# Routing between the attention tasks of bodies 1 to 3, token rows sent from body 4 on, on one NeuronCore

## The chip, the cores and the metric

The kernel runs on one core of a Trainium2 chip. The core has five engines that run side by side: TensorE (PE in the profile, its weight loads PEld), VectorE (DVE), ScalarE (ACT), GpSimd (POOL), and SyncE (SP), which here only issues DMAs. The metric is the device time of one execution in microseconds (us), as a median of several runs; less is better.

## The reference, cut to what matters

The input is 8 sequences of 512 tokens with 128 features. After a layer norm, an attention layer (32 query heads, 16 key/value heads, ALiBi bias, causal) and a mixture of experts read the same normed tokens; the result is x + attention * silu(experts). The experts part decides where each token goes from eight gate logits:

```python
gate_logits = x @ gate_w + gate_b
topk_vals, topk_idx = jax.lax.top_k(gate_logits, K)     # K = 2 of E = 8
topk_w = jax.nn.softmax(topk_vals, axis=-1)
comb = jnp.sum(onehot * topk_w[..., None], axis=2)
h = gelu(jnp.einsum('btd,edf->ebtf', x, w1) + b1)
y = jnp.einsum('ebtf,efd->ebtd', h, w2) + b2
output = jnp.einsum('ebtd,bte->btd', y, comb)
x = x + attention(xn) * silu(output)
```

The kernel does not compute all eight experts for every token. It sorts tokens into blocks of 256 slots, each block of one expert, computes the blocks, and gathers each token's two results.

## The kernel before, in words

**Stages.** There is a preamble (loads, layer norm, transposes, weights split in high and low halves, gate logits), then 32 attention bodies, then the expert blocks, then 32 more attention bodies, and the final sum. A body is two key/value heads of one sequence. In the first 32 bodies the tokens also go out to memory in slot order (`slot_x`): one tile of 128 tokens a body. The experts read `slot_x` and write `slot_y`; the last 32 bodies fetch rows of `slot_y`.

**Order.** No scheduler decides anything at run time: each engine runs its own list in order, and semaphores join them. `ORDER` (L70) gives for each engine and half a table of tasks (name, body offset, place in per cent of a window). `one_window` (L315) runs one window: a task with offset 1 works for the next body. `enter_bodies` (L338) runs the two windows before the first, `run_bodies` (L344) the rest, the first four and the last four written out and those between as a loop of two windows, `leave_bodies` what remains.

**Tasks.** On PE, M are twelve rough score products a body, from which DVE takes row maxima (B, twelve a body, `peaks`, L1382); C turns these shifts (L887); S are the ten groups of scores (L904 to L913); P the ten groups of values (L936 to L940); K, Q, V and O are projections. ACT takes exponentials (E, L1180), copies shifts (C, L1169) and splits high halves; DVE subtracts to get low halves (Q, K, V, A) and divides by the sum (N). POOL subtracts for each exponential group its low half (L, `lo_part`, L781: one instruction of 128x512), which P of the same group waits for. Group 9 of a body is L9 on POOL and P9 on PE. The O projection lags by two bodies.

**Choosing and routing.** While the windows before body 0 run, DVE does the top-2 choice in three steps behind B1, B3 and B5 (`choose`, L1365). Then, between `enter_bodies` and the first window: PE multiplies the choices with a triangle and with ones to rank the tokens of each expert (33 matmuls, L991 and L994, into columns of PSUM bank 4, which the values tasks use later); ACT does one exponential (L1233) with an activation table load before and one behind; DVE waits for the exponential and the ranks and does the routing in 27 instructions without a break (L1478 to L1519), each followed by a wait for its own end (`small`). It ends with `routed`. PE's first values task waits for `routed` (L920).

**Sending rows.** For a tile of 128 tokens, ACT copies the high halves (R, `send_hi`, L1199), POOL subtracts the low halves and copies the two slot numbers of each token (I0, I1, `send_ready`), and issues two indirect DMAs (D0, D1, `send`, L758). `sent_with` (L463) says which tiles belong to a body: tile n-2 in bodies 2 to 29, tiles 28 and 29 in body 30, 30 and 31 in body 31. There are two buffers, by the tile's parity; R and I0 wait until the last tile of their buffer has landed. R stands at 72 per cent of window n-2, I0 at 82 of window n-2, I1 at 34, D0 at 62 and D1 at 75 of window n-1.

## Time and profile before

| | |
|---|---|
| median of 3 runs | 1255.06 us (1253.67 to 1255.94) |
| the profiled execution: time, span | 1253.06 us, 1251.1 us |
| busy, share of the span | PE 92%, DVE 80%, ACT 75%, POOL 70% |
| share of time of the DMA queue of the hardware rings | 54.7% |
| mean granted TensorE clock | 0.981 |

The page of the profile also has the span in 40 slices, groups of instructions by line with their mean duration and the wait before them, and DMA issues. A timeline row is: start in us, length in us, engine, line, operation, output<-input and shapes, count, and in brackets the idle time of the engine just before, with what ended it. A row of busy time gives, for one stretch, how long each engine was busy in it.

### The profile page before, as it was taken

The numbers are of one execution on the slowest core, as the hardware profiler recorded it, in microseconds if no ns is written. First come the engines' busy times: TensorE is split into PE (matmuls) and PEld (weight loads), VectorE is DVE, ScalarE is ACT, GpSimd is POOL, SyncE is SP. The second block draws the span as 40 slices with busy tenths as digits, with TensorE's granted clock in tenths as the row PEclk, the third lists the DMA queues.
The fourth block names the chain that finished last, engine by engine and source line by source line (L and its number), as shares of the span: only waits on it lengthen the run. The fifth ranks groups of instructions, "written<-read, shape, count | busy, mean of one in ns | idle before, by whom it ended". The sixth has DMA issues, their size and how long they took to land. (4 is left out here: it accounts for less than half of the span.)

```text
span 1251.1 us, 52908 instructions
## 1 busy us (share of the span) xinstructions
PE 1154.0 (92%) x17226; PEld 912.5 (73%) x17226; DVE 1005.5 (80%) x3099; ACT 939.0 (75%) x1807; POOL 878.3 (70%) x1086
## 2 busy tenths in 40 slices
PE   2579999999999999987999779999999999999994
PEld 0357777777777777766888657777777777777873
DVE  8778888888888888764777648888888888888885
ACT  2468888888888888775666458888888888888884
POOL 9048888888888888875000058888888888888885
PEclk9989999999999999999999979999999999999997
DMA  8326666666666666644433456555555555555663
GB/s 243 158 57 144 143 147 151 143 143 144 144 144 144 144 143 143 147 107 86 87 90 86 94 129 141 136 135 134 134 134 134 134 134 134 134 134 134 138 139 95
DMA packets 286161, 165.28 MB, mean 132 GB/s; under 512 B 174994, under 2 KB 274674, under 8 KB 285428
## 3 DMA queue, kind: packets, MB, share of 16 engines
q1 hardware_dynamic: 281972, 155.63, 54.7%
q0 software_dynamic: 4096, 8.40, 2.3%
q8 instruction: 59, 0.97, 0.3%
q14 instruction: 34, 0.28, 0.1%
HBM read 15.76 MB, written 16.78 MB: 26 GB/s over the span
## 5 line engine op out<-in xcount | busy, mean ns | idle before, releaser
L781 POOL TENSOR_TENSOR t_lo<-stage 128x512 f16<-128x512 f32 x640 | 654.4, 1038 | 148.7 <-ACT stage L1180 144.5
L1392 DVE CUSTOM_DVE_ANT_0 stage<-ps,kmask 128x512 bf16<-128x512 f32 (+3 forms) x1024 | 466.2, 488 | 110.7 <-PE ps L878 91.9
L1180 ACT ACTIVATE stage<-ps,slope 128x512 f32<-128x512 f32 (+1 forms) x768 | 456.8, 620 | 126.8 <-PE ps L913 80.7
L904 PE MATMUL ps<-q_st,k_st 128*128 128x256 f16 (+3 forms) x1024 | 302.5, 301 | 4.0 <-DMA k_st<-stage 1.8
L936 PE MATMUL outs<-v_sp,stage 128*128 128x65 f16 x2560 | 283.3, 194 | 12.2 <-DVE stage L1422 9.0
L938 PE MATMUL outs<-v_sp,stage 128*128 128x64 f16 x2560 | 283.1, 194 | 0.0
L940 PE MATMUL outs<-v_sp,t_lo 128*128 128x65 f16 x2560 | 283.0, 194 | 0.0
L878 PE MATMUL ps<-k_st,stage 128*128 128x512 f16 (+3 forms) x1024 | 252.8, 304 | 14.9 <-DVE spread L1392 7.6
L936 PEld LDWEIGHTS outs<-v_sp,stage 128*128 128x128 bf16 x2560 | 239.4, 98 | 21.5 <-issue 11.2
L938 PEld LDWEIGHTS outs<-v_sp,stage 128*128 128x128 bf16 x2560 | 236.5, 98 | 8.9 <-issue 0.3
L940 PEld LDWEIGHTS outs<-v_sp,t_lo 128*128 128x128 f16 x2560 | 236.5, 98 | 0.0
L905 PE MATMUL ps<-q_st,k_st 128*128 128x128 f16 x1024 | 224.0, 219 | 0.0
L908 PE MATMUL ps<-q_st,k_st 67*128 67x384 f16 (+2 forms) x768 | 211.5, 275 | 0.0
L1169 ACT CAST q_st<-ps 1x512 f16<-1x512 f32 x256 | 147.9, 578 | 32.5 <-PE ps L887 27.2
L913 PE MATMUL ps<-late_q,late_k 66*128 66x134 f16 (+1 forms) x640 | 136.0, 212 | 0.0
L904 PEld LDWEIGHTS ps<-q_st,k_st 128*128 128x128 f16 x1024 | 100.4, 98 | 34.7 <-issue 14.3
L734 POOL COPY slot_now<-slot_of 128x1 uint32 (+1 forms) x128 | 23.2, 183 | 144.6 <-DMA slot_y<-stage 144.6
L878 PEld LDWEIGHTS ps<-k_st,stage 128*128 128x128 f16 x1024 | 84.3, 98 | 53.0 <-issue 24.3
L1125 ACT ACTIVATE stage<-ps,qscale 128x512 f16<-128x512 f32 x128 | 88.5, 691 | 44.9 <-PE ps L816 36.9
L905 PEld LDWEIGHTS ps<-q_st,k_st 128*128 128x128 f16 x1024 | 100.4, 98 | 17.2 <-issue 0.6
L908 PEld LDWEIGHTS ps<-q_st,k_st 67*128 67x128 f16 x768 | 74.8, 97 | 51.7 <-issue 1.9
L1422 DVE TENSOR_TENSOR stage<-outs,stage 128x512 f16<-128x512 f32 x128 | 88.0, 687 | 21.7 <-ACT stage L1160 21.7
(205 smaller groups left out, 2702.1 us busy)
## 6 DMA issues: line engine op xcount, KB each, us to landing
k_st<-stage SPq DMA_DIRECT2D x256, 128.0 KB, 2.4
q_st<-stage SPq DMA_DIRECT2D x256, 128.0 KB, 2.4
q_st<-stage SPq DMA_DIRECT2D x256, 64.0 KB, 2.1
k_st<-stage SPq DMA_DIRECT2D x128, 64.0 KB, 2.1
slot_y<-stage SPq DMA_DIRECT2D x40, 128.0 KB, 2.0
X<-in_L_attn_inputs SPq DMA_DIRECT2D x8, 512.0 KB, 8.0
slot_x<-att SPq DMA_DIRECT2D x2, 2048.0 KB, 8.7
wx_raw<-in_L_ffn_w SPq DMA_DIRECT2D x64, 64.0 KB
```

What stands on the lines that cost most here:

```text
L781: pool.tensor_tensor(t_lo[r], t_p[r], upper(t_p[r]), ALU.subtract).then_inc(s[f"lo{u % NG}"], 1)
L878: mm = pe.matmul(M_ps[h][:, c0:c0 + w], q_raw[sl][:, 0, i * P:(i + 1) * P], k_st[par][sl][:, 2 + h, 0:w], start=True, stop=True)
L904: pe.matmul(d, k[:, 0, at], q[:, 0, seen], start=(c0 == 0), stop=False, skip_group_check=True)
L905: pe.matmul(d[:, 0:P], k[:, 1, at], q[:, 1, at], start=False, stop=True, skip_group_check=True)
L908: pe.matmul(d[:, P:], k[far, 1, at], q[far, 1, (kt + 1) * P:SEQ], start=False, stop=True, skip_group_check=True)
L913: pe.matmul(d, late_k[late, :], late_q[late, LATE:P].unsqueeze(1).to_broadcast([P - LATE - 1, len(first), P - LATE]), start=False, stop=Tr ...
L936: pe.matmul(d, p_hi, v[:, with_one], start=(opens and i == kt), stop=False, skip_group_check=True)
L938: pe.matmul(d[:, OUT_COL[sl]:OUT_COL[sl] + DH], p_hi, v[:, lo], start=False, stop=False, skip_group_check=True)
L940: mm = pe.matmul(d, t_lo[r][:, c], v[:, with_one], start=False, stop=(closes and i == QT - 1), skip_group_check=True)
L1169: ins = act.copy(q_st[sl][h][DH:DH + 1, 1, :], M_ps[0][SHIFT[h]:SHIFT[h] + 1, :])
L1180: e = act.activation(t_p[r][:, c0:c1], S_ps[u % 2][:, c0:c1], ACT.Exp, scale=slope[:, bass.ds(pair_index(n) * 2 * SLOTS + sl * 2 + h, 1)])
L1392: ins = dve.tensor_tensor_reduce(junk[h][:, c0:c0 + w], M_ps[h][:, c0:c0 + w], kmask[:, SEQ - w:SEQ], -1.0 / 1024, 3e38, ALU.add, ALU.min, ...
```

## The change

1. `run_bodies`: the first half now writes out windows 0 to 17 and 30, 31 and loops over 18 to 29 (before: written out 0 to 3 and 28 to 31). The second half writes out its first four and last two.
2. The 33 rank matmuls are called on PE behind V0 of body 1 in window 0 (`ranks`). ACT, behind E4 of body 0, copies ranks and totals out of PSUM (`keep_ranks`); PE's first values task waits for these copies (`kept`) and no more for `routed`.
3. The 27 routing instructions on DVE are cut in eight steps (`route`), run behind B3 and B5 of body 1, N0 of body 0, B3 and B5 of body 2, N0 of body 1, B3 and B5 of body 3. They read the copies, not PSUM.
4. The activation table for Exp is loaded once, before the odd tiles are normed, and not around L1233.
5. Rows are sent from body 4 on: tile 0 with body 4, one a body, two in bodies 7, 10, 13 and 16 (the first of them through a third buffer), so that from body 17 on tile n goes with body n and body 31 sends one. R stands at 0 of the window and no more at 72.

```diff
-            ("E0", 0, 4), ("E1", 0, 8), ...
+            ("R0", 2, 0), ("E0", 0, 4), ("E1", 0, 8), ...
-            ("E7", 0, 71), ("R0", 2, 72), ("A0", 0, 76), ...
+            ("E7", 0, 71), ("A0", 0, 76), ...
-                if "Y" in tasks and name in CHOICE:
-                    tasks["Y"](n, 0, CHOICE[name])
-        CHOICE = {"B1": 0, "B3": 1, "B5": 2}
+                if "Y" in tasks and isinstance(n, int) and (name, n) in FIRST_ONES[engine_name]:
+                    tasks["Y"](FIRST_ONES[engine_name].index((name, n)))
+        FIRST_ONES = {"DVE": [("B1", 0), ("B3", 0), ("B5", 0), ("B3", 1), ("B5", 1), ("N0", 0), ("B3", 2), ("B5", 2),
+                              ("N0", 1), ("B3", 3), ("B5", 3)],
+                      "PE": [("V0", 1)], "ACT": [("E4", 0)]}
-            start, end = lo + 2 * UNROLL, hi - 2 * UNROLL
+            start, end = lo + (max(TWICE) + UNROLL if lo == 0 else 2 * UNROLL), hi - UNROLL
+        rank_of, total_of = L, t1[:, 0, :]
-        def sent_with(n):
+        FIRST_SENT, TWICE = 4, (7, 10, 13, 16)
+        def sent_with(n, par):
             if not isinstance(n, int):
-                return [n - UNROLL]
-            return [t for t in range(NT) if min(t + UNROLL, HALF - UNROLL + (t - NT) // 2 + UNROLL) == n]
+                return [(n, par, (n - FIRST_SENT) // UNROLL)]
+            if n < FIRST_SENT:
+                return []
+            t = n - FIRST_SENT + len([b for b in TWICE if b <= n])
+            more = [(t - 1, UNROLL, TWICE.index(n))] if n in TWICE else []
+            return more + [(t, n % UNROLL, (n - FIRST_SENT) // UNROLL)]
...
-                    pe.wait_ge(s["routed"], 1)
+                    pe.wait_ge(s["kept"], 2)
...
+            def keep_ranks(_):
+                act.wait_ge(s["ranked"], 1)
+                act.copy(rank_of, ps[4][...]).then_inc(s["kept"], 1)
+                act.copy(total_of, ps[4][...]).then_inc(s["kept"], 1)
```

The steps of `route` (the instructions are those of L1478 to L1519 in their order): step 0 is L1478 to L1480; 1 waits for `kept` and is L1483 to L1489; 2 is L1491 to L1494; 3 is L1497 to L1499; 4 is L1500 to L1505; 5 the four of L1508 and L1509; 6 is L1511 and L1512; 7 is L1514 to L1519.

## Rows read from the trace of the kernel before

**Rows 1.** Two stretches: length, busy PE, PEld, DVE, ACT, POOL, PE clock, DMA.
```profile
189.70:220.80 31.10, 30.92 (x490) 24.73 (x488) 27.00 (x87) 26.03 (x52) 27.01 (x33) 1.00 0.66 152
82.65:115.00 32.35, 31.10 (x484) 23.50 (x483) 26.81 (x92) 27.26 (x52) 25.83 (x31) 1.00 0.60 125
```

**Rows 2.** Timeline, window 1: K0 and end of B6 on DVE, M8 on PE.
```profile
101.66 0.69 DVE L1407 SCALAR_TENSOR_TENSOR stage<-ps,stage 128x512 f16<-128x512 f32 x1 [0.48 <-ACT stage L1133]
...
102.87 0.09 DVE L1392 DVE_READ_ACCUMULATOR2_ANT spread<- 128x1 f16 x1
...
103.10 0.38 PE L878 MATMUL ps<-k_st,stage 128*128 128x128 f16 x2
```

**Rows 3.** Timeline of POOL: a window with one tile, and one with two.
```profile
504.19 1.01 POOL L758 DMA_INDIRECT slot_x<-row_now,slot_now  x1 [0.15 <-issue]
...
506.45 0.98 POOL L758 DMA_INDIRECT slot_x<-row_now,slot_now  x1 [0.17 <-issue]
...
509.60 4.02 POOL L781 TENSOR_TENSOR t_lo<-stage 128x512 f16<-128x512 f32 x4
...
538.35 1.01 POOL L758 DMA_INDIRECT slot_x<-row_now,slot_now  x1 [0.15 <-issue]
...
543.15 0.96 POOL L758 DMA_INDIRECT slot_x<-row_now,slot_now  x1 [0.31 <-issue]
```

**Rows 4.** Timeline of PE: the first matmul of P9 after the one-tile window.
```profile
511.71 0.19 PE L936 MATMUL outs<-v_sp,stage 128*128 128x65 f16 x1
```

**Rows 5.** Timeline of PE around the routing.
```profile
62.96 0.42 PE L991 MATMUL outs<-chosen,tri 128*128 128x264 f16 x1
...
66.32 0.38 PE L904 MATMUL ps<-q_st,k_st 128*128 128x512 f16 x1
...
76.28 0.59 PE L887 MATMUL ps<-ident,spread 128*128 128x128 f16 x4 [8.71 <-DVE spread L1392]
```

**Rows 6.** Timeline of ACT: its V0 task, once a body.
```profile
112.16 0.60 ACT L1140 ACTIVATE v_sp<-ps 128x512 f16<-128x512 f32 x1
...
143.13 0.60 ACT L1140 ACTIVATE v_sp<-ps 128x512 f16<-128x512 f32 x1
...
251.90 0.64 ACT L1140 ACTIVATE v_sp<-ps 128x512 f16<-128x512 f32 x1
...
500.60 0.64 ACT L1140 ACTIVATE v_sp<-ps 128x512 f16<-128x512 f32 x1
...
534.79 0.63 ACT L1140 ACTIVATE v_sp<-ps 128x512 f16<-128x512 f32 x1
...
555.85 0.63 ACT L1140 ACTIVATE v_sp<-ps 128x512 f16<-128x512 f32 x1
```

**Rows 7.** Timeline of DVE, routing instructions.
```profile
64.83 0.18 DVE L1478 TENSOR_SCALAR top<-top 128x32 f32<-128x32 f32 x1 [0.94 <-ACT top L1233]
...
67.93 1.02 DVE L1494 TENSOR_SCALAR per_e<-per_e 128x8 f32<-128x8 f32 x1
68.99 1.28 DVE L1497 TENSOR_TENSOR wx_lo<-wx_lo,per_e 128x320 f32<-128x320 f32 x1
...
75.14 0.23 DVE L1519 TENSOR_TENSOR slot_of<-slot_of,slot_bits 128x64 uint32<-128x64 uint32 x1
```

**Rows 8.** Timeline of POOL in the same stretch.
```profile
67.88 2.04 POOL L781 TENSOR_TENSOR t_lo<-stage 128x512 f16<-128x512 f32 x2 [36.37 <-ACT stage L1180]
```

**Rows 9.** Timeline of ACT: the second R in body 31's pair.
```profile
544.88 0.30 ACT L1204 CAST row_now<-mix 128x128 f16<-128x128 f32 x1 [4.25 <-DMA slot_x<-row_now,slot_now]
```

**Rows 10.** Who PE waited for from 560 to 572 us: total, times, longest.
```profile
PE outs L936 <- POOL t_lo L781: 1.5, 3, 0.9
```

**Rows 11.** Timeline of POOL: the low half of a tile that is sent.
```profile
507.46 0.44 POOL L746 TENSOR_TENSOR row_now<-mix,row_now 128x128 f16<-128x128 f16 x1
```

**Rows 12.** DMAs that write or read `slot_x`, from issue to landing.
```profile
DMA to landing us min/median/max: 3.0/3.4/12.8
```

**Rows 13.** Timeline of ACT: E0 and E1 at a window's start.
```profile
510.39 1.35 ACT L1180 ACTIVATE stage<-ps,slope 128x512 f32<-128x512 f32 x2 [0.62 <-PE ps L913]
```

More of the change, by code:

```diff
@@ L420, in weights_split, with over_e @@
             eng.wait_ge(s["wlo"], len(SPLITS))
+        L, t1, one1, L2, one2, cw = (lg[:, i, :, :] for i in range(6))
+        rank_of, total_of = L, t1[:, 0, :]
+        def over_e(a):
+            return a.unsqueeze(2).to_broadcast([P, NT, E])
+        ev = eidx[:, :].unsqueeze(1).to_broadcast([P, NT, E])
         RANK = E * FC
@@ L736, in send_ready @@
             def send_ready(n, par, k):
-                for i, t in enumerate(sent_with(n)):
-                    at = t % UNROLL if isinstance(t, int) else par
+                for t, at, used in sent_with(n, par):
                     if isinstance(t, int) and (t, k) == (0, 0):
@@ L750, in send @@
             def send(n, par, k):
-                for t in sent_with(n):
-                    at = t % UNROLL if isinstance(t, int) else par
+                for t, at, _ in sent_with(n, par):
                     pool.wait_ge(s["ready0"], t * 2 + 2)
@@ L1199, in send_hi @@
             def send_hi(n, par, _):
-                for t in sent_with(n):
-                    at = t % UNROLL if isinstance(t, int) else par
-                    need(act, f"sent{at}", t // UNROLL * 32)
+                for t, at, used in sent_with(n, par):
+                    need(act, f"sent{at}", used * 32)
                     act.copy(row_now[at][:, 0:D], mix[:, bass.ds(t, 1), :].rearrange("p a d -> p (a d)"))\
@@ L1221, in _ @@
             roots(1, QT, NT)
+            act.preload_act_table(ACT.Exp)
             act.wait_ge(s["norm"], 1)
@@ L1474, in _ @@
             dve.wait_ge(s["attz"], 1)
-            enter_bodies("DVE", {**tasks, "Y": lambda n, _, k: choose(k)}, 0, HALF)
-            dve.wait_ge(s["topexp"], 1)
-            small(dve.tensor_scalar(top[:, 6, :], top[:, 5, :], WS, WS, ALU.mult, ALU.add))
-            small(dve.reciprocal(top[:, 6, :], top[:, 6, :]))
-            small(dve.tensor_tensor(top[:, 7, :], top[:, 6, :], top[:, 5, :], ALU.mult))
-            blocks, first, end, first_slot = (per_e[:, i, :] for i in range(4))
-            small(dve.tensor_scalar(ecmp[:, :, :], ecmp[:, :, :], 0.0, None, ALU.is_gt))
@@ L1484, in _ @@
-            dve.wait_ge(s["ranked"], 1)
-            total = ps[4][:, RANK + NT * E:RANK + (NT + 1) * E]
-            over = scratch[:, 0:TOK // BLK * E].rearrange("p (e j) -> p e j", e=E)
-            small(dve.tensor_tensor(over, total.unsqueeze(2).to_broadcast([P, E, TOK // BLK]), steps[:, :, :],
-                                    ALU.is_gt))
-            small(dve.tensor_reduce(blocks, over, AX_X, ALU.add))
-            before = scratch[:, 0:E * E].rearrange("p (e f) -> p e f", e=E)
-            small(dve.tensor_tensor(before, blocks.unsqueeze(1).to_broadcast([P, E, E]), ecmp[:, :, :], ALU.mult))
@@ L1492, in _ @@
-            small(dve.tensor_reduce(first, before, AX_X, ALU.add))
-            small(dve.tensor_tensor(end, first, blocks, ALU.add))
-            small(dve.tensor_scalar(first_slot, first, float(BLK), None, ALU.mult))
-            ended = scratch[:, :].rearrange("p (b e) -> p b e", e=E)
-            small(dve.tensor_tensor(ended, block_no[:, :, :], end.unsqueeze(1).to_broadcast([P, NBLK, E]), ALU.is_ge))
-            small(dve.tensor_reduce(blk_f[:, :], ended, AX_X, ALU.add))
-            small(dve.tensor_scalar(blk_f[:, :], blk_f[:, :], E - 1.0, None, ALU.min))
@@ L1523, in _ @@
             dve.wait_ge(s["zeros"], 16 * ZERO_DMAS)
-            run_bodies(dve, "DVE", tasks, 0, HALF)
+            run_bodies(dve, "DVE", {**tasks, "Y": lambda k: route(k - CHOICES)}, 0, HALF)
             leave_bodies("DVE", tasks, 0, HALF, late=LATE_O)
```

114 lines of the change are left out of this document (72 added, 42 removed), and 4 rows, old and new, of the table ORDER.

## The prediction, as written before the result

> **What bounds the kernel now.** I read the busy times by stretch first. In the middle of the first half two bodies take 31.1 us, in which PE is busy 30.9, DVE 27.0, POOL 27.0 and ACT 26.0 [rows 1]. So in a settled body every microsecond that PE waits is lost, and the next two engines have some 2 us of slack a body. That slack isn't free to use, because the lists are fixed: in window 1 DVE ends B6 at 102.96 and PE starts M8, which needs it, at 103.10 [rows 2]. DVE delivers 0.1 to 0.2 us ahead of its use, so a delay there comes out on PE nearly one for one. POOL is as tight at one place: it ends four L groups (L8, L9, L0, L1, one every 1.0 us) from 509.60 on, so L9 ends at 511.6, and P9 starts at 511.71 [rows 3, 4]. Two places stand out from the settled state: the start, where PE idles 8.71 us until 76.28 because DVE is routing [rows 5], and the last windows of the first half, where the bodies get longer [rows 6]. The change touches both, and moves work into the tight bodies for it.
>
> **Part 1, the start.** PE ranks from 62.96 to 66.32 (3.36 us), does S0, M11 and S1, and idles until C1 at 76.28 [rows 5]. C1 needs B10 and B11, which stand behind the routing on DVE. With the routing gone, DVE is free at 63.9 (where it begins to wait for L1478), PE goes from 62.96 straight to S0, S1 takes the place of the ranks, and C1 comes at about 65.4: it needs M11 behind S0 (0.9 us at the slow clock, twice the time it has behind the ranks), then B11 and S1. That is 10.9 us earlier. The removed table loads are what lets E0 follow S0; they have no price of their own. After an idle stretch PE runs at 1.2 GHz for a while; the four matmuls of C1 at 76.28, 128 columns each, start 0.1 us apart, the pace of that clock, and with the idle gone this costs some 1 us less (an estimate: two of three slow microseconds, each half lost). Against that stand, in window 0, the 33 rank matmuls, now at 2.4 GHz, about 2.0 us (half of 3.36 and a little), and P0's wait for ACT's copies (`kept`), about 0.6 us (two short PSUM copies of 0.4 and 0.2 behind the last matmul, in part under M3). ACT waits for the ranks with the high half of V0 and E5 queued behind; their users come after P0 or later, so they cost nothing more, and SP's list is only told to count a third semaphore at the half's end, where all has landed. Gain: 10.9 + 1.0 - 2.0 - 0.6 = **9.4 us**. If window 0 is held by something else as well, it is less; the floor is the 8.7 us of idle less 2.6, so 6.1.
>
> **Part 2, the routing inside bodies 1 to 3.** The routing instructions run from 64.83 to 75.37 [rows 7]. Of these 10.5 us, 0.7 is a wait for the ranks and 1.7 another kind of wait: L1494, on 8 elements a partition, took 1.02 us where its like take 0.2, and L1497, on 320, took 1.28 where its length asks 0.4; they end at 68.95 and 70.27, and POOL runs two L groups from 67.88 to 69.92 [rows 7, 8]. So 8.0 us are the instructions' own. These go onto a DVE that has 0.1 us of lead over PE. What is absorbed is the idle time right behind a step: all but 0.2 of step 0, while PE waits for the copies, and some 0.5 in front of the K0 task (0.48 in window 1 [rows 2]) in each of three windows, some 2.3 us in all; an estimate of 2.5 with the gaps of 0.1 elsewhere. Left: **5.5 us lost** (bounds 2.5, if all of the 5.5 us that DVE idles from 82.65 to 115 [rows 1] is used, and 8.0).
>
> Then the POOL waits. In the old place POOL had two instructions in the whole routing. From 82.65 to 115 it is busy 25.8 of 32.35 us, some 6 of them with sends that are gone from there [rows 1, 3]: 60%, in pieces of 1.04 us. Of the 27 routing instructions some 20 have two inputs in SBUF or the form of L1494. Bounds: nothing, if all fall in POOL's gaps, and 20 x 1.04 = 20.8 us, if each meets an L group at its start. I laid the steps on POOL's row: step 3 falls mostly in a gap, steps 1, 2, 4, 5 and 7 meet one or two groups each. That is some 5.5 us. I take **5.5**, nearer the lower end, since POOL's groups come in bursts and a DVE stall holds ACT and with it POOL back. Each stall of 2 us or more on PE also brings a few us at 1.2 GHz, as the last windows show: body 31 grows by 5.5 us for a wait of 4.25 [rows 6, 9]. I add **1 us**. Part 2 costs 12.0 us; parts 1 and 2 together lose 2.6 us.
>
> The SBUF page of the Trainium skill ("SBUF — State Buffer", section "Who interferes with whom") speaks against this part: VectorE and GpSimd share one pair of SBUF ports as an exclusive lock, which a VectorE instruction with two SBUF inputs, or in a 2-port mode, takes for its whole length, while a tensor_reduce never does. 
>
> **Part 3, the end of the half.** V0 marks a body. From 251.90 to 500.60 sixteen bodies take 15.54 us each; the two bodies from there to 534.79 take 34.19, 3.1 too long, and the next, to 555.85, takes 21.06, 5.5 too long [rows 6]. ACT's R waits for the indirect DMAs of its buffer, 4.25 us for body 31, and with ACT the A task and PE's P5 behind it [rows 9]. The change has no pair left there. Behind the second pair's four DMAs PE waits 1.5 us for POOL in one window more [rows 10]; I count 2.1 with waits too short for a row. Gain: 3.1 + 5.5 + 2.1 = **10.7 us** (bounds 9 and 11.5).
>
> **Part 4, four pairs in bodies 7, 10, 13 and 16.** The third buffer takes away the wait on the partner, not POOL's work. In a window with one tile, D1 starts 2.26 us after D0; with two, the last D starts 4.80 after the first [rows 3]. So L7, L8 and L9 come 2.5 us later, and L9 has 0.1 of lead [rows 3, 4]: PE loses about 2.3 us, close to what rows 10 show. The window before has a second L746 (0.44, [rows 11]) and a slot copy ahead of the same L9: 0.45 more. 4 x 2.75 = **11.0 us lost** (bounds 4 x 1.5 = 6, rows 10 alone, and 4 x 3.2 = 12.8). R at 0 of the window waits for the landing of the D1 in the window before, which takes 3.0 to 3.4 us from its start [rows 12]: 506.45 + 3.2 = 509.65, and R's turn, in front of E0, is from 509.77 on, with 0.62 us of idle to follow [rows 13], so it costs nothing in plain bodies. Behind a pair it comes 2.5 us later; E0 and S2 behind it are delayed by less than P9 delays PE anyway. If that cover goes, it costs up to 2 us a pair, and more than one tile in a row would show it.
>
> **Part 5, loops and sends.** Written out, two bodies took 30.97 us (112.16 to 143.13), in the loop 31.09 [rows 6]. Fourteen more bodies written out in the first half, two fewer at the end of each half: 5 x 0.1 = 0.5 us gained (bounds 0 and 2). No sends in windows 1 and 2 spares 0.3. Together **0.8**.
>
> **Sum.** 9.4 - 12.0 + 10.7 - 11.0 + 0.8 = -2.1: the kernel gets 2.1 us slower. On the profiled execution's 1253.06 us (span 1251.1 and 2.0 around it) that is 1255.2; this execution lies 2.0 us under the median of 1255.06, so the median becomes **1257.2**. A measurement tells 0.2%, 2.5 us, from no change: under 1252.5 is faster, over 1257.6 slower.
>
> **Rivals.**
> A. The routing slips into POOL's gaps. For it: step 0 and 3 do, and the reduces between them were not held up by POOL. Then 5.5 and 1.0 us of part 2 fall away: 1257.2 - 6.5 = 1250.7. Against it: POOL 60% busy.
> B. The routing meets POOL at nearly every instruction. For it: both instructions that ran beside POOL in rows 7 were held. At 13 us of waits instead of 5.5 it is 1264.7, slower. The point from which it decides: over 6 us of waits the whole is over 1257.6.
> C. The pairs cost only what rows 10 show, 1.5 us each, since POOL's idle time around them takes the rest: 11.0 - 6.0 = 5 us less, 1252.2. Against it: POOL's idle time stands ahead of D0, not behind it.
> D. The written-out bodies are fetched slower than the loop, or R at 0 stalls ACT in every body by 0.1 to 0.2 us over 28 bodies: 4 us more, 1261. Nothing in rows 6 shows it for the four windows that are written out now.
>
> **How the numbers follow.** Forecast 0.38 (of it 0.21 within 0.2%, 0.12 slower, 0.05 faster); A 0.22 (0.19 faster, 0.03 same); B 0.22, slower; C 0.10 (0.07 faster, 0.03 same); D 0.08, slower. Faster 0.31, same 0.27, slower 0.42. The range goes from 1247 (A with a part of C) to 1265 (B).
>
> **What the profile of the changed kernel would show.** PE without the 8.7 us idle, and C1 of body 0 near 65.4 instead of 76.28; routing instructions of two SBUF inputs at 0.2 to 0.5 us in gaps and over 1 us beside L781; bodies 2 and 3 (V0 to V0) of 17 to 20 us; bodies 30 and 31 of 15.5; PE waiting on L781 about 2.3 us in the windows behind the D tasks of bodies 7, 10, 13 and 16. Wrong is the prediction if bodies 1 to 3 stay near 15.5 us, if the pair windows do, or if the loop-free windows have a length of their own.

## The result, and the profile after

The changed kernel takes **1246.86 us** (median of 6, 1243.65 to 1248.89) where the kernel before takes 1254.37 (median of 6, 1251.46 to 1256.17). The ratio is 0.994, with an interval of 0.9921 to 0.9959: faster by 7.5 us. Two further comparisons of the same kernels, on two chips, gave 0.9932 and 0.9935 (below), so the sign and the size are settled. The forecast was 1257.2 and "slower by 2.1", in a range from 1247 to 1265: the direction was wrong, and the time lies just under the range.

The profiled execution of after took 1248.89 us with a span of 1247.1, that of before 1253.06 with 1251.1. So the two traces differ by 4.0 us in span, the medians by 7.5. The profiled execution of after is the slowest of its six, and that of before lies 1.3 us under its median; 2.0 and 1.3 make up nearly all of the difference. So a ledger of these two traces can place 4.0 us and no more; the rest is looked for in the medians and the further traces of the experiments.

First the ledger. ACT's V0 task marks a body, as in [rows 6]; from here on V5 is the start of V0 in body 5, and "V5 to V18" the stretch between two such marks. In the timeline of ACT of the kernel after (start, length, engine, line, operation, in brackets the idle time ahead):

```profile
72.39 0.62 ACT L1160 ACTIVATE v_sp<-ps 128x512 f16<-128x512 f32 x1
89.35 0.63 ACT L1160 ACTIVATE v_sp<-ps 128x512 f16<-128x512 f32 x1
107.99 0.63 ACT L1160 ACTIVATE v_sp<-ps 128x512 f16<-128x512 f32 x1
125.68 0.63 ACT L1160 ACTIVATE v_sp<-ps 128x512 f16<-128x512 f32 x1
140.97 0.64 ACT L1160 ACTIVATE v_sp<-ps 128x512 f16<-128x512 f32 x1
...
171.85 0.63 ACT L1160 ACTIVATE v_sp<-ps 128x512 f16<-128x512 f32 x1
...
189.65 0.63 ACT L1160 ACTIVATE v_sp<-ps 128x512 f16<-128x512 f32 x1
```

Body 1 begins at 72.39, the three bodies behind it take 16.96, 18.64 and 17.69 us, the next 15.29, and the body from 171.85 on, with a pair of tiles, 17.80. The whole ledger, with what the prediction had for each place:

| stretch, by V0 marks | before | after | gained | predicted |
|---|---|---|---|---|
| start to V1 | 81.63 | 72.39 | +9.24 | +9.4 (part 1) |
| V1 to V4 (routing) | 46.32 | 53.29 | -6.97 | -12.0 (part 2), +0.3 |
| V4 to V29 (four pairs, written out) | 387.93 | 398.66 | -10.73 | -11.0 (part 4), +0.5 |
| V29 to V32 (end of the half) | 178.81 | 168.49 | +10.32 | +10.7 (part 3) |
| V32 to V33 (start of the second half) | 53.10 | 51.32 | +1.78 | 0 |
| V33 to the end of the span | 503.31 | 502.95 | +0.36 | 0 |
| sum | | | +4.00 | -2.1 |

In this pair of traces three of the four large terms came within 0.4 us of the prediction. That close is luck in part: further traces of the same two kernels move single stretches by 1 to 2 us (e0, e10, e12). The fourth, the routing inside the tight bodies, was priced at 12.0 and cost 7.0. Its rows on DVE, to be held against [rows 7] (first column start, second length):

```profile
74.99 1.12 DVE L1416 TENSOR_TENSOR wx_lo<-wx_lo 128x128 f32<-128x128 f32 x1
76.15 0.29 DVE L1418 TENSOR_REDUCE per_e<-wx_lo 128x8 f32<-128x128 f32 x1
...
93.00 0.70 DVE L1432 CAST blk_word<-word_f 1x5 uint32<-1x5 f32 x1
...
108.99 0.31 DVE L1441 CAST slot_of<-slot_f 128x64 uint32<-128x64 f32 x1
...
110.40 0.97 DVE L1445 TENSOR_SCALAR slot_bits<-slot_of 128x64 uint32<-128x64 uint32 x1
111.41 0.96 DVE L1447 TENSOR_SCALAR slot_of<-slot_of 128x64 uint32<-128x64 uint32 x1
112.40 0.22 DVE L1449 TENSOR_TENSOR slot_of<-slot_of,slot_bits 128x64 uint32<-128x64 uint32 x1
```

and POOL in the same stretches:

```profile
74.93 2.09 POOL L799 TENSOR_TENSOR t_lo<-stage 128x512 f16<-128x512 f32 x2 [3.70 <-ACT stage L1200]
...
91.65 2.04 POOL L799 TENSOR_TENSOR t_lo<-stage 128x512 f16<-128x512 f32 x2 [1.03 <-ACT stage L1200]
...
110.28 2.04 POOL L799 TENSOR_TENSOR t_lo<-stage 128x512 f16<-128x512 f32 x2 [1.03 <-ACT stage L1200]
```

L1445 begins 0.12 us behind POOL's first group and ends at 111.37, when that group (half of 2.04) is over; L1447 meets the second group and ends at 112.37, 0.05 behind it; the cast L1432 ends at 93.70, the group at 93.69. L1418, a tensor_reduce, runs in its own 0.29 us beside POOL's second group. The eight steps, from the start of the first instruction of each to the end of its last, add up to 11.06 us where their own time is 8.0: the waits for POOL are **3.1 us**, not 5.5: nearly all of it in four instructions (L1416, L1432, L1445, L1447).

What PE waited for from 75 to 125 us (total, times, longest; a fourth row, 0.2 us for ACT, is left out):

```profile
PE ps L832 <- DVE stage L1471: 5.0, 3, 2.2
PE ps L896 <- DVE spread L1463: 0.7, 2, 0.6
PE ps L905 <- DVE spread L1463: 0.7, 1, 0.7
```

The delay arrives where the prediction put it, at PE behind DVE, and most of it, three times, at one place: the bank that DVE frees with L1471.

### The profile page after: what moved, and what is told of

Same layout as the page of the kernel before. It is cut to its first block and busy times, and to the rows that moved or that the text cites. A ratio compares the mean times of both kernels' runs of the same rounds, so it can differ in the third digit from the quotient of the medians.

```text
span 1247.1 us, 52099 instructions
## 1 busy us (share of the span) xinstructions
PE 1153.4 (92%) x17226; PEld 910.2 (73%) x17226; DVE 1005.9 (81%) x3099; ACT 939.9 (75%) x1808; POOL 877.8 (70%) x1086
## 3 DMA queue, kind: packets, MB, share of 16 engines
q8 instruction: 79, 1.29, 0.5%
## 5 line engine op out<-in xcount | busy, mean ns | idle before, releaser
L896 PE MATMUL ps<-k_st,stage 128*128 128x512 f16 (+3 forms) x1024 | 252.7, 304 | 15.5 <-DVE spread L1463 8.4
L922 PEld LDWEIGHTS ps<-q_st,k_st 128*128 128x128 f16 x1024 | 100.6, 98 | 33.3 <-issue 11.5
L1283 ACT ACTIVATE X<-ps,b1T 128x256 f32<-128x256 f32 x160 | 66.9, 471 | 45.4 <-PE ps L834 45.4
```

What stands on the lines that cost most here:

```text
L896: mm = pe.matmul(M_ps[h][:, c0:c0 + w], q_raw[sl][:, 0, i * P:(i + 1) * P], k_st[par][sl][:, 2 + h, 0:w], start=True, stop=True)
L922: pe.matmul(d, k[:, 0, at], q[:, 0, seen], start=(c0 == 0), stop=False, skip_group_check=True)
```

## The experiments

Most executions of a kernel lie within 2 us of their median, single ones 5 or 6 above it, and the kernel before took 1254.1, 1257.8, 1259.1 and 1260.6 us on four of the chips used here. So times are compared on one chip or by their ratio to the kernel before. Stretches are taken from V0 marks; how far those repeat is told under e0 and e10. Lines of an edit that are left out are marked by `...`.

**e0: the changed kernel again, beside the next three.**

> The changed kernel once more, for a second profile and to compare with the other runs on one chip. Theory 1 (the gain is the sum of terms that come back each time: start 2.2 us, last windows of the half 10.3, pairs -9.4): 4 to 8 us under the kernel before, four pair bodies (V0 to V0) of 17.8 us. Theory 2 (a part of the 7.5 us is the clock of single executions): the distance to before goes under 4 us, and the fourth pair body, 19.05 in the first profile, and the start of the second half move by over 1 us.

Measured: 1246.88 us (4 runs) against 1254.07, ratio 0.9932 [0.9915, 0.995]. The V0 marks of bodies 1, 4 and 5 lie within 0.13 us of those of the first trace. The four pair bodies take 17.93, 18.20, 19.24 and 17.64 us, where the first trace has 17.80, 17.81, 17.85 and 19.05. So the whole comes back, as theory 1 says, and yet single bodies move by more than 1 us, as theory 2 says. Why one pair body or another takes 1.4 us more is open.

**e1: the routing back in one piece ahead of the bodies.** All else stays: pairs in bodies 7 to 16, windows written out, no pair at the end.

```diff
-FIRST_ONES = {"DVE": [("B1", 0), ("B3", 0), ("B5", 0), ("B3", 1), ("B5", 1), ("N0", 0), ("B3", 2), ("B5", 2),
-                      ("N0", 1), ("B3", 3), ("B5", 3)],
-              "PE": [("V0", 1)], "ACT": [("E4", 0)]}
+FIRST_ONES = {"DVE": [("B1", 0), ("B3", 0), ("B5", 0)], "PE": [], "ACT": []}
...
-                    pe.wait_ge(s["kept"], 2)
+                    pe.wait_ge(s["routed"], 1)
 # PE, before its bodies
+ranks(0)
 # ACT, before its bodies
+act.preload_act_table(ACT.Exp)
+keep_ranks(0)
 # DVE, before its bodies
+for k in range(8):
+    route(k)
```

> The changed kernel with the ranks, their copies, the routing and the table loads back in one piece between enter_bodies and the first window; sends and written-out windows stay changed. Theory 1 (spreading gains 9.2 us at the start and loses 7.1 in bodies 2 to 4, and the rest is the sends): 2 us slower than the changed kernel, bodies 2 to 4 near 15.0 to 15.5 us, V0 of body 1 at 81.6. Theory 2 (the prediction's sum): 2.6 us faster than the changed kernel. Theory 3 (the gain of the change is in the start alone): as slow as before.

Measured: 1251.15 us, ratio 0.9977 [0.9967, 0.9987]: 4.3 us above e0. In its trace V1 to V4 are

```profile
83.14 0.60 ACT L1160 ACTIVATE v_sp<-ps 128x512 f16<-128x512 f32 x1 [0.32 <-PE ps L833]
98.14 0.63 ACT L1160 ACTIVATE v_sp<-ps 128x512 f16<-128x512 f32 x1
113.68 0.60 ACT L1160 ACTIVATE v_sp<-ps 128x512 f16<-128x512 f32 x1
128.29 0.63 ACT L1160 ACTIVATE v_sp<-ps 128x512 f16<-128x512 f32 x1
```

V1 is at 83.14, 1.5 us later than in the kernel before. Only 0.2 of that is there when C1 of body 0 starts (76.48 against 76.28). The rest is PE's clock behind the idle stretch, in the rows of one microsecond (length, busy PE, PEld, DVE, ACT, POOL, then PE's granted clock, DMA share, GB/s), first of the kernel before, then of e1:

```profile
80.00:81.00 1.00, 1.00 (x14) 0.82 (x13) 0.70 (x4) 0.77 (x2) 1.00 (x2) 1.00 0.00 0
```

```profile
80.00:81.00 1.00, 1.00 (x4) 0.43 (x3) 0.90 (x4) 0.00 (x0) 1.00 (x2) 0.50 0.02 8
```

The clock is back at 1.00 from 79.4 us on in the kernel before, and from 82.2 on in e1. But this isn't e1's own: in the second trace of the kernel before (e10) C1 starts at 75.74, the clock comes back at 81.6 and V1 is at 82.45, and in e9, with the same start, V1 is at 82.60. The slow stretch lasts 3 us in some executions and nearly 6 in others.

By the medians the moved routing is worth 4.3 us, known to about 2 us. The ledger of the first two traces has 9.24 - 6.97 = 2.3, e1's trace against that of the changed kernel 10.75 - 8.14 = 2.6, and the prediction had a loss of 2.6. So theory 2 is out, and theory 1 has the sign.

V1 to V4 is 45.15 us here. The kernel before has 46.32 and 46.62 in its two traces and 45.61 and 46.36 in e2 and e9, which are the same code up to there (windows 0 to 3 were written out already). So the missing sends spare 0.5 to 1.5 us, 1.2 against the first trace, and not 0.3. Against this base the routing costs 53.29 - 45.15 = **8.1 us**.

**e2 and e9: only the windows written out.** The kernel before, with windows up to 17 of the first half written out instead of looped.

```diff
-start, end = lo + 2 * UNROLL, hi - 2 * UNROLL
+start, end = (18 if lo == 0 else lo + 2 * UNROLL), hi - 2 * UNROLL
```

> The kernel before with windows 0 to 17 written out in the first half in place of 0 to 3, nothing else. Theory 1 (a loop turn costs 0.1 us): 0.5 to 1 us under before, which is the same. Theory 2 (the loop's branch costs several tenths a turn and is what the change gains by): 3 us or more under before.

Measured: 1248.65 us (5 runs, 1247.65 to 1253.38), ratio 0.9954 [0.994, 0.9968]. By this, writing out alone would bring 5.4 of the 7.2 us. But the trace shows 2.4 us from V5 to V18 (202.04 to 199.67 us), and 1.9 lost again from V29 to V31. So it was run again.

> The kernel before with bodies 5 to 17 written out instead of looped, once more. Theory 1, that writing out brings what the first medians said (5.4 us): ratio 0.994 to 0.997 again. Theory 2, that it brings what the trace shows of these bodies (202.0 to 199.7 us, 2.4) and the rest was chance in which executions fell together: ratio 0.997 to 0.9985. The trace should show bodies 5 to 17 at 199.7 us under either.

Measured: 1257.36 us (10 runs) against 1259.14, ratio 0.9989 [0.9973, 1.0005], above both theories' windows. That is 1.8 us by the medians, and the interval reaches from nothing to 3.4 us, while that of e2 reaches from 4.0 to 7.5: the two don't meet. Between them lie the two pairs of traces: from V1 to V31, 474.2 to 473.4 us in one pair and 475.4 to 472.1 in the other, so 0.8 and 3.3 us. Writing out probably brings between 1 and 5 us. The predicted 0.5 is low by all four figures, but the interval of e9 doesn't exclude it, and nothing here narrows it further.

**e10: the kernel before, profiled a second time.**

> The kernel before, unchanged, for a second trace of it. If the ledger between the traces of before and after can be trusted to a few tenths of a us at each place, bodies 2 to 4 take 46.3, bodies 5 to 17 202.0, the last two before the end of the half 40.0, the start of the second half 138.8 and 53.1, and only those two last differ by up to 1.5 us, since the clock falls at other moments. If not, other places differ by over 0.5 us. The one execution lies at 1251 to 1257 us.

Measured: 1260.28 us, span 1258.3. V1 to V4 took 46.6 us, V29 to V31 39.1, the start of the second half 138.8 and 53.1: as in the first trace within 1.0. But V1 came at 82.45 instead of 81.63 (see e1), V5 to V18 took 203.6 instead of 202.0, and V33 to V62 457.6 instead of 452.8. So a single row of the ledger is good to 1 or 2 us and not to tenths. The last figure goes with the chip: e0 to e3, on one chip, have 452.8 to 453.8 there, and the traces of e4 to e13, on three others, 456.0 to 458.1, and e14 and e15, on a fifth, 452.8 and 452.3.

**e3 and e7: the second tile's work at places of its own.** In a window with a pair, POOL's work for the second tile (low half, two indices, two DMAs) stands in the lists at other places, behind L4, and no longer behind the first tile's.

```diff
+("H0", 2, 50), ("J0", 1, 50), ("J1", 0, 50),     # POOL's list, between L4 and L5
...
 def send_ready(n, par, k):
-    for t, at, used in sent_with(n, par):
+    for t, at, used in sent_with(n, par)[-1:]:
...
 def send(n, par, k):
-    for t, at, _ in sent_with(n, par):
+    for tile in sent_with(n, par)[-1:]:
```

> The changed kernel, but the second tile of bodies 7, 10, 13 and 16 gets POOL places of its own: its low half and slot numbers in front of L5 of window n-2, one indirect DMA in front of L5 of window n-1, the other in front of L5 of window n, where POOL waits about 1 us for ACT. Theory 1 (a pair costs 2.4 us because four indirect DMAs stand between D0 and L9, behind which POOL has no idle time until L2): the pair bodies fall to 15.4 to 15.8 us and the kernel is 7 to 9 us faster than the changed one. Theory 2 (POOL's total work is the limit, wherever it stands): the same cost shows in the neighbouring bodies, total within 2 us of the changed kernel.

Measured: **1236.33 us**, ratio 0.9858 [0.9842, 0.9875], 10.55 us under e0. V5 to V17 is 185.10 us against 196.09 in the changed kernel, 11.0 less, and no body of it is longer than 16.02. So theory 1 holds, with more gained than its 7 to 9 us, and part 4 of the prediction (11.0 us for the four pairs) is confirmed in cause and size. The spread pairs aren't quite free: with the same windows written out and no pair, e2 and e9 have 184.71 and 184.47 us there. The view of waits for the first pair's window in the changed kernel, 171.85 to 189.65 us, reads

```profile
PE outs L954 <- POOL t_lo L799: 1.9, 3, 0.9
```

and in e3, from 171 to 187, it has no row at all. What stands ahead of those waits is in POOL's timeline of the changed kernel:

```profile
175.42 1.01 POOL L776 DMA_INDIRECT slot_x<-row_now,slot_now  x1 [0.15 <-issue]
176.73 0.96 POOL L776 DMA_INDIRECT slot_x<-row_now,slot_now  x1 [0.30 <-issue]
177.72 1.05 POOL L799 TENSOR_TENSOR t_lo<-stage 128x512 f16<-128x512 f32 x1
178.93 0.98 POOL L776 DMA_INDIRECT slot_x<-row_now,slot_now  x1 [0.17 <-issue]
180.22 0.96 POOL L776 DMA_INDIRECT slot_x<-row_now,slot_now  x1 [0.30 <-issue]
```

Each issue holds POOL for 1.0 us plus 0.15 to 0.30: the last begins 4.80 us behind the first, as [rows 3] has it, and the next L group waits.

> The kernel in which each second tile's work lies at places of its own in the window, timed once more beside the next one. If the 11 us between it and the changed kernel are real, the ratio to the kernel before is again 0.984 to 0.988 and bodies 6 to 17 together take 185 us in the trace, against 196 in the changed kernel. If the earlier figure was luck of the chip, the ratio lies nearer 0.990.

Measured: 1241.09 us against 1259.14, ratio 0.9866 [0.9839, 0.9892], V5 to V17 at 185.57 us. The gain belongs to the kernel.

**e5: R at its old place.** In the changed kernel R stands first in ACT's window and in pair windows it waits for the row buffer to be free.

```diff
-("R0", 2, 0), ("E0", 0, 4),
+("E0", 0, 4),
-("E7", 0, 71), ("A0", 0, 76),
+("E7", 0, 71), ("R0", 2, 72), ("A0", 0, 76),
```

> The changed kernel with ACT's R task back at 72 per cent of the window. Theory 1 (R's wait for landings behind a pair, 2.1 and 3.3 us in the profile, is covered by PE's wait for L9): within 1 us of the changed kernel (1247), pair bodies 17.8. Theory 2 (R's wait is a part of the pairs' price): pair bodies 17 or less and 3 us faster.

Measured: ratio 0.9922 [0.9897, 0.9948], within the interval of the changed kernel. In the changed kernel's timeline of ACT the wait in the first pair's window is

```profile
184.06 0.30 ACT L1223 CAST row_now<-mix 128x128 f16<-128x128 f32 x1 [3.28 <-DMA slot_x<-row_now,slot_now]
```

four such waits come to 11.5 us (2.1 to 3.3 each), and in e5 there is none. Yet the pair bodies last as long, 17.66 against 17.80 us for the first, and V5 to V17 takes 197.53 us against 195.3 to 196.7 in the three traces of the changed kernel. So a wait of 3.3 us in the trace was worth 0.1 at most: ACT waited while PE waited for POOL anyway. Part 4 had said so ("delayed by less than P9 delays PE anyway").

**e6: all windows of the first half written out, on top of e3.**

```diff
-start, end = lo + (max(TWICE) + UNROLL if lo == 0 else 2 * UNROLL), hi - UNROLL
+start, end = (hi - UNROLL if lo == 0 else lo + 2 * UNROLL), hi - UNROLL
```

> e3_pair_spread with all 32 windows of the first half written out, no loop in it. Theory 1 (a written-out body is 0.1 to 0.2 us shorter than one in the loop, 15.36 against 15.54 in the run with windows written out alone, and entering the loop costs about 0.9 once): 1.5 to 3 us faster than e3_pair_spread (1236.3), so 1233.5 to 1235. Theory 2 (written-out bodies gain by something else, such as where code lies): no faster.

Measured: 1239.51 us on another chip, ratio 0.9847 [0.9825, 0.9869], against e3's 0.9858: 1.4 us by the ratios, well inside the intervals. In the traces V5 to V31 is 401.0 us against 402.4. Twelve more bodies written out give 0.1 us each in this pair, within what traces differ by.

**e4: the price of a small DVE instruction in a tight body.** Four instructions of 128x64 are added behind B5 in each of the 12 looped bodies; once with two inputs in SBUF, once with one.

```diff
+if j == 5 and not isinstance(n, int) and bodies_of_half[0] == 0:
+    for i in range(4):
+        dve.tensor_tensor(idle_out[:, i, :], idle_in[:, 0, :], idle_in[:, 1, :], ALU.add)
 # or, in e4_one_input
+        dve.tensor_reduce(idle_out[:, i, 0:8], idle_in[:, 0, :].rearrange("p (a b) -> p a b", b=8), AX_X, ALU.add)
```

> The changed kernel with four more VectorE instructions behind B5 in each of the twelve loop bodies 19 to 30 (added work, its output unused): tensor_tensor, 128x64 in float32, both inputs in SBUF. Alone such an instruction takes 0.23 us. Theory 1 (the shared port is what the routing waited for, and it can be met in the bodies at about half of the instructions at most): mean 0.35 to 0.6 us each, single ones over 1 us, the loop bodies 1.2 to 2.2 us longer. Theory 2 (the prediction's 5.5 us on 20 instructions, 0.28 us each, is right): mean about 0.5 and bodies over 2 us longer. Theory 3 (no such wait in settled bodies): 0.23 each, bodies 0.8 us longer.

> The same with four tensor_reduce, 128x64 to 128x8, one input in SBUF, 0.22 us each alone (added work, output unused). Theories 1 and 2: never held by GpSimd, all at 0.22 to 0.25 us, loop bodies 0.7 to 0.9 us longer than in the changed kernel, since VectorE has 0.1 us of lead. Theory 3 as well. If VectorE's idle time of 2 us a body can be used after all, the bodies stay at 15.54.

Measured, in the view of the added tile (duration of one in ns, min/median/max), for two inputs and then for one:

```profile
L1472 DVE TENSOR_TENSOR idle_out<-idle_in x48: 217/221/1073, 370.1 to 555.9; 128x64 f32<-128x64 f32 x48
```

```profile
L1472 DVE TENSOR_REDUCE idle_out<-idle_in x48: 206/210/216, 368.5 to 544.8; 128x8 f32<-128x64 f32 x48
```

V19 to V31, twelve looped bodies, is 202.14 us with two inputs, 191.76 with one, and 186.65 in the changed kernel: 1.29 and 0.43 us more a body. With one input the four take 0.59 us from the first start to the last end, since they overlap; with two inputs 1.48:

```profile
370.07 1.48 DVE L1472 TENSOR_TENSOR idle_out<-idle_in 128x64 f32<-128x64 f32 x4
371.47 0.74 DVE L1477 SCALAR_TENSOR_TENSOR stage<-ps,qscale,stage 128x512 f16<-128x512 f32 x1
```

```profile
370.43 1.04 POOL L802 TENSOR_TENSOR t_lo<-stage 128x512 f16<-128x512 f32 x1 [1.27 <-ACT stage L1203]
```

One of them meets POOL's group, 370.43 to 371.47, and lasts to its end. So of four instructions in a row just one waits, 0.85 us, and the others are through before or after it: a sequence waits once for each POOL group that it meets, not once per instruction. Theory 1 has the size (0.37 us each in the mean, single ones over 1 us, 1.29 a body).

**e11, e14, e15: which instructions wait.** Two instructions of the routing's last step, which took 0.97 and 0.96 us, have one input. So tensor_scalar was put at the place of e4.

```diff
+        dve.tensor_scalar(idle_out[:, i, :], idle_in[:, 0, :], P - 1, 2, ALU.bitwise_and, ALU.logical_shift_left)
```

> The changed kernel with four tensor_scalar of 128x64 uint32 (one SBUF input, the form of the routing's last steps) added behind B5 in each of the 12 bodies that are looped in the first half (19 to 30); their output isn't used. Four tensor_tensor there took 1.48 us a body (one of them 1.07 where its own time is 0.22) and made a body 1.32 us longer; four tensor_reduce with one input never waited (206 to 216 ns) and cost 0.45 us a body. Theory 1, that only two SBUF inputs make VectorE wait for GpSimd: every tensor_scalar takes 190 to 220 ns and the bodies are 0.4 to 0.5 us longer than in the changed kernel. Theory 2, that tensor_scalar waits as well, as the 0.97 and 0.96 us of the routing's last steps say: the longest take about 1 us, at least one in four waits, and the bodies are 1.1 to 1.4 us longer.

Measured: 186 to 192 ns each, V19 to V31 at 190.61 us, 0.33 more a body. It tells nothing on the question: the four began at 370.87, the last of them before POOL's group did at 371.23. Eight were needed.

> The changed kernel with eight tensor_scalar of 128x32 uint32 (one SBUF input) behind B5 in each of the 12 looped bodies of the first half; their output isn't used. Four of them were through 0.05 us before GpSimd's next L group had begun, so they tested nothing; eight reach into it. Theory 1, that tensor_scalar with one input waits for GpSimd as one with two inputs does: one of the eight in each body takes 0.8 to 1.2 us and ends with GpSimd's group, and the bodies are 1.2 to 1.8 us longer than in the changed kernel (15.55). Theory 2, that it never waits and something else held the routing's last steps: all eight take 0.15 to 0.22 us, and the bodies are 0.6 to 1.0 us longer.

> The same with eight tensor_reduce of 128x32 float32 (one SBUF input) in their place; their output isn't used. Both theories: none waits, all take 0.15 to 0.22 us though several lie beside GpSimd's group, and the bodies are 0.6 to 1.2 us longer. If one takes over 0.8 us, the kind of the instruction doesn't matter and only the place does.

Measured, eight tensor_scalar and then eight tensor_reduce:

```profile
L1472 DVE TENSOR_SCALAR idle_out<-idle_in x96: 168/175/1029, 369.3 to 557.7; 128x32 uint32<-128x32 uint32 x96
```

```profile
L1472 DVE TENSOR_REDUCE idle_out<-idle_in x96: 172/176/183, 369.8 to 548.8; 128x4 f32<-128x32 f32 x96
```

Eight tensor_scalar take 1.63 us from 369.33 on, with POOL's group from 369.69 to 370.75; eight tensor_reduce take 0.83 us from 369.83 on beside a group from 370.19, and none lasts over 183 ns. The bodies are 16.98 and 16.15 us: 0.83 apart, the wait. Theory 1 holds for the instruction: tensor_scalar with one SBUF input waits for POOL, tensor_reduce doesn't, at the same place. The bodies grew by 1.43 us and by 0.60, as had been expected. The two also differ in type, uint32 against float32; L1494 in [rows 7], a tensor_scalar of float32 values, took 1.02 us beside POOL as well.

**e8 and e13: the routing in 15 steps where DVE idles.** On top of e6: a step behind N0 of body 0, then one behind each Q0, N1 and N0 of windows 1 to 5, and rows sent from body 7 on, with seven pairs.

```diff
-FIRST_ONES = {"DVE": [("B1", 0), ("B3", 0), ("B5", 0), ("B3", 1), ("B5", 1), ("N0", 0), ("B3", 2), ("B5", 2),
-                      ("N0", 1), ("B3", 3), ("B5", 3)],
+FIRST_ONES = {"DVE": [("B1", 0), ("B3", 0), ("B5", 0), ("N0", 0), ("Q0", 2), ("N1", 0), ("N0", 1), ("Q0", 3), ("N1", 1), ("N0", 2), ("Q0", 4),
+                      ("N1", 2), ("N0", 3), ("Q0", 5), ("N1", 3), ("N0", 4), ("Q0", 6), ("N1", 4)],
-FIRST_SENT, TWICE = 4, (7, 10, 13, 16)
+FIRST_SENT, TWICE = 7, (10, 13, 16, 19, 22, 25, 28)
...
```

> The kernel with all windows of the first half written out and its second tiles at places of their own, and now the routing cut in 15 steps, one behind each of the tasks N0, Q0, N1 of bodies 0 to 4, where VectorE stands idle; rows are sent from body 7 on, so there are seven windows with two tiles. Theory 1, that what the routing costs is VectorE time in windows where VectorE ends last, so that it matters where it stands: the bodies 2 to 6 lose only what doesn't fit the idle gaps, and together with body 1 take 3 to 5 us less than the same stretch with eight steps (V0 of body 6 at 156.2 in the kernel with eight steps, 151 to 153 here); median 3 to 5 us lower, ratio 0.980 to 0.982. Theory 2, that the gaps are waits for TensorE and move along with whatever is put into them: V0 of body 6 at 155 to 157 and the ratio within 0.002 of the kernel with eight steps (0.9847), or above it if the three further windows with two tiles cost something.

Measured: 1237.98 us, ratio 0.9847 [0.9816, 0.9878], 3.1 us under e7 on the same chip. Its marks V1 to V6:

```profile
71.51 0.62 ACT L1183 ACTIVATE v_sp<-ps 128x512 f16<-128x512 f32 x1
88.04 0.60 ACT L1183 ACTIVATE v_sp<-ps 128x512 f16<-128x512 f32 x1 [0.55 <-PE ps L857]
103.57 0.60 ACT L1183 ACTIVATE v_sp<-ps 128x512 f16<-128x512 f32 x1
119.12 0.60 ACT L1183 ACTIVATE v_sp<-ps 128x512 f16<-128x512 f32 x1
134.78 0.60 ACT L1183 ACTIVATE v_sp<-ps 128x512 f16<-128x512 f32 x1
151.57 0.60 ACT L1183 ACTIVATE v_sp<-ps 128x512 f16<-128x512 f32 x1 [0.54 <-PE ps L857]
```

V6 is at 151.57 against 156.19 in e6, inside theory 1's 151 to 153: three of the bodies with routing take 15.5 to 15.7 us, two take 16.5 and 16.8. Of these 4.6 us 0.8 lies ahead of V1, where no routing stands in either and where traces with that start range from 70.5 to 72.5. V1 to V6 is 80.06 against 83.88, 3.8 less. A part of it may be the sends of bodies 4 to 6, which e8 has later (for two bodies e1 puts them at 0.5 to 1.5 us). At V31, where both have sent as many tiles, V1 to V31 is still 2.4 us shorter, three more pairs included.

The waits for POOL aren't fewer: over their own time the routing instructions of e8 lose 3.4 us to them by their rows, against 3.1 in eight steps. What the 15 places change must then be how much of the routing and its waits DVE's idle time takes in; that is inferred from these two figures. The ratio came out above theory 1's 0.980 to 0.982, so the medians leave it open on that chip, and the traces decide for theory 1.

> The changed kernel once more, unchanged, on this chip. Theory 1, that the ratio belongs to the kernels: 0.992 to 0.996 again. Theory 2, that part of it belongs to the chip, as the two ratios of the written out bodies alone (0.9954 and 0.9989) suggest: under 0.991 or over 0.997. By the traces' ledger alone (1251.1 to 1247.1 us) the ratio would be 0.9968.

> The kernel with the routing in 15 steps in VectorE's idle time, once more, now beside the changed kernel on one chip. If what the traces show holds (4.6 us at body 6, 11 us for the second tiles' places), it lies 11 to 15 us under the changed kernel: ratio to the kernel before 0.981 to 0.985. If its lead over the kernel with eight steps was chance, 8 to 11 us under: 0.985 to 0.988.

Measured: the changed kernel 1252.78 us, ratio 0.9935 [0.9917, 0.9954], as before (theory 1), with V1 to V4 at 54.60 us in its trace, 1.3 more than in the other two; the kernel with 15 steps **1238.71 us, ratio 0.9831 [0.9813, 0.9848]**, 14.1 us under it on the same chip. It beats both kernels, the changed one (e12) by 1.1%. Against the kernels with spread pairs and eight steps (ratios 0.9866 and 0.9847) the intervals overlap. V6 lies at 151.54 again.

## Why the prediction went wrong

**Part 1 was right**: 9.4 predicted (its terms add up to 9.3), 9.24 in the ledger. With the longer slow stretch of e10 and e9 it would have been about 10. C1 of body 0 was put at 65.4 and came at 65.14, right behind S1; the ranks take 2.05 us (predicted 2.0), and P0 waits 0.29 us (predicted 0.6) for ACT's copies. In the timeline of PE:

```profile
65.14 0.38 PE L905 MATMUL ps<-ident,spread 128*128 128x128 f16 x4
...
69.98 2.05 PE L1014 MATMUL outs<-chosen,ones 128*128 128x256 f16 x32
...
72.56 0.21 PE L954 MATMUL outs<-v_sp,stage 128*128 128x65 f16 x1 [0.29 <-ACT wx_lo L1260]
```

**Part 2 is the step that failed**, in size and not in kind: priced at 12.0 us, it cost 7.0 in the ledger, and 6.7 to 8.3 over all traces of the two kernels. Its terms, one by one:
- 8.0 us of own time: right.
- The port waits: 5.5 predicted, 3.1 measured. I counted "one or two groups each" for steps 1, 2, 4, 5 and 7. Steps 2 and 5 met none; steps 1 and 4 met one each (0.88 and 0.54 us over their own time), step 7 two that stood back to back (0.77 and 0.76), and steps 3 and 6 the last 0.1 us of one. The kinds of instructions that wait were right (e14, e15); how often the steps would meet a group was not.
- Clock: 1 us was put down. PE's granted clock from V2 to V3 was 0.91 in the trace of after, and from 89 to 108 us 1.00 in e8; that body, 18.64 us, is the longest of the three. 0.09 of 18.64 is 1.7 us at most, so this term was roughly right in size. Its reason, that each stall of 2 us or more brings slow microseconds, didn't hold: behind the wait of 1.47 us that ends at 95.01 the clock was at 0.50 from 96 to 99 us, and behind the wait of 2.23 us that ends at 113.60 it stayed at 1.00.
- Absorbed: 2.5 predicted. 8.0 + 3.1 + (0 to 1.7) less the measured 8.1 leaves 3.0 to 4.7. This is a remainder and stands in no row: more was hidden than I took, if the other terms are right, with 5.5 us of DVE idle time in the stretch as the bound.
- The sends that are gone from there: 0.3 predicted, 1.2 measured (e1 against the first trace of the kernel before; 0.5 to 1.5 against all four with that start).

These make 12.0 - 0.3 = 11.7 into 7.0. The two that count most are the waits, 2.4 us too high, and what was absorbed, 0.5 to 2.2 us too low. With part 2 alone set right the sum is a gain of 2.6 where it was a loss of 2.1, and the forecast 1252.5: the direction is right, the size still 5.6 us short.

**Parts 3 and 4 were right.** The end of the half brought 10.3 (predicted 10.7). Spreading the four pairs gave back 11.0 by e3's trace and 10.55 by its median (predicted 11.0). What they are made of was right as well: POOL's issues of 1.0 us each push L7 to L9 and so P9 back, and R's wait, though 2 to 3 us long, costs nothing (e5).

**Part 5** was probably low: 0.5 for the windows, between 1 and 5 by e2 and e9, without a firm lower end.

**The rest** lies outside the sum. The start of the second half gave 1.78 us in the ledger, which nothing in the change explains. One and the same kernel gave 52.26 us for it in one trace and 49.07 in the other (e3, e7), and the rows of stretches there (length, then busy PE, PEld, DVE, ACT, POOL, then PE's granted clock, DMA share, GB/s) show why. In e3

```profile
720.00:732.00 12.00, 12.00 (x136) 8.47 (x136) 7.14 (x25) 7.06 (x13) 8.42 (x9) 0.76 0.22 50
```

and in e7

```profile
720.00:732.00 12.00, 11.93 (x171) 8.85 (x170) 8.83 (x32) 8.33 (x15) 9.04 (x10) 0.92 0.26 64
```

PE idles there a few times for 1 to 3 us, and its clock is down for longer in one than in the other: 136 matmuls or 171 in the same 12 us. And 3.3 us are the distance of the two profiled executions from their medians, on opposite sides. The further traces place a part of it: V33 is at 747.8 and 749.7 us in the two of the kernel before and at 744.2, 743.5 and 742.6 in the three of the changed kernel, 5.3 apart in the mean and not the 3.6 of the first pair. The rest of it stays open.

Of the **rivals**, A (1250.7) came nearest. It took all port waits and the clock's term out of part 2, 6.5 us, and was right in direction, but not for its own reason: in fact 3.1 us of waits came, and the difference lay as much in what the idle time absorbed. B asked for over 6 us of waits, and 3.1 came. C had the pairs at 1.5 us each, and they cost 2.75. D was wrong in its sign: written out, a body is 0.2 to 0.3 us shorter (V5 to V18 in e2 and e9 against the two traces of before), and R at 0 costs nothing (e5).

**The range** ended at 1247, from rival A and a part of C, and the result is 1246.86. The bounds that the text itself gave reach further: waits at nothing (-5.5), 5.5 us absorbed (-3.0) and the windows at 2 (-1.5) make 1247.2 with the pairs at their full price, and 1242.2 with the pairs at their lower bound of 6. What it didn't hold at all is that the start of the second half moves by 2 to 3 us from one execution to the next, and that the median of the kernel before is itself known to 1 or 2 us only.

By the page "SBUF — State Buffer" of the Trainium skill, section "Who interferes with whom", copy, cast and tensor_scalar can enter modes that take both port pairs and so contend with GpSimd, a tensor_tensor with two inputs in SBUF does so with its reads, and a tensor_reduce never does on this chip. The traces agree for the four kinds that ran beside POOL here: 0.70 us for a cast of five elements that takes 0.16 alone, 0.96 and 1.029 us for tensor_scalar (0.20 and 0.175), 1.073 for tensor_tensor (0.22), and 183 ns at most for tensor_reduce (0.176).

## What to carry to other kernels

Price small instructions on a shared port by how many of the other engine's instructions the whole sequence meets, not by how many of its own instructions can wait. Where a fixed list alternates between engines, look for the places where the engine in question idles already, and put work there in pieces as short as the idle time; here 15 pieces in the idle places instead of eight behind the tight tasks, with the sends begun later, took 3.8 us off the first bodies and 2.4 off the half. And when doubled work must go into a window, put the second share where the queue has slack, since four DMA issues in a row cost 2.75 us a window and the same four spread out 0.3 at most.

## What the runs showed of the hardware

- An indirect DMA's issue holds GpSimd for 0.96 to 1.01 us, with 0.15 to 0.30 of idle ahead of each (first pair's rows above); spread apart, they fit in idle time.
- The chips differ in the second half: V33 to V62 takes 452.3 to 453.8 us on two chips and 456.0 to 458.1 on three others, with PE's granted clock at 1.00 on both (in the two traces of the kernel before, 915 to 1070 us). The difference is spread thin, most bodies 0 to 0.3 us longer; its cause is open. So the kernel before took 1254.1 us on one chip and 1260.6 on another, while three ratios of the changed kernel lie within 0.001. That isn't so for every kernel: the written-out windows alone gave 0.9954 and 0.9989.
- The granted clock in a row isn't always the pace at which the matmuls run, and its mean doesn't rank kernels. In e3's trace it is at 0.50 from about 20 to 60 us, and in e0's at 1.00, first e3, then e0:

```profile
35.00:45.00 10.00, 7.20 (x102) 5.32 (x102) 7.47 (x16) 7.52 (x15) 0.00 (x0) 0.50 0.69 290
```

```profile
35.00:45.00 10.00, 7.21 (x85) 5.32 (x86) 7.43 (x19) 8.01 (x16) 0.00 (x0) 1.00 0.70 292
```

  But PE is busy for 18.4 us between 20 and 60 us in both, with 177 matmuls in each. And e0's matmuls of 512 columns start 0.43 us apart at 61 us and 0.22 apart at 68 us, with 1.00 in the rows of both:

```profile
61.07 0.63 PE L832 MATMUL ps<-xT_hi,wq_hi 128*128 128x512 f16 x1
61.49 0.63 PE L833 MATMUL ps<-xT_lo,wq_hi 128*128 128x512 f16 x1
...
67.94 0.38 PE L832 MATMUL ps<-xT_hi,wq_hi 128*128 128x512 f16 x1
68.16 0.38 PE L833 MATMUL ps<-xT_lo,wq_hi 128*128 128x512 f16 x1
```

  The first distance is the pace of 1.2 GHz, the second that of 2.4. So e0 ran this stretch as slowly as e3, whatever its row says, and the lower mean clock of e3's execution (0.965 against 0.984 in e0), nearly all of which comes from here, says nothing of its time.
